# Transposes of two key blocks back to back in a causal attention kernel, value matmuls in pairs

## The chip, the cores and the metric

One core of one Trainium2 chip runs the whole program. The metric is the device time of one execution in microseconds (µs). Engines are named as in the profile: PE (TensorE, matmuls and transposes), PEld (its weight loads), DVE (VectorE), ACT (ScalarE), POOL (GpSimd), SP (the queue that issues the DMAs).

## The reference, cut to what matters

A layer norm with modulation, grouped causal attention, and a gated feed-forward part. The change touches the attention alone:

```python
qkv = einsum('bsh,ph->bsp', x, weight_qkv)       # b=2, s=1024, 4 kv groups, 4 query heads each, d=128
scores = einsum('bsgqd,btgd->bgqst', q, k) * scale
scores = where(causal, scores, min)
attn = softmax(scores, axis=-1)
out = einsum('bgqst,btgd->bsgqd', attn, v)
return einsum('bse,he->bsh', out, weight_proj)
```

## The kernel before

A program written by hand for each engine, with semaphores between them. The attention is a loop of 8 turns (batch x kv group, `t` = 0 to 7). Float32 products are made of two parts, a high one (`_hi`, type fp32r) and the rest (`_lo`), in three matmuls each (`three`, L801 to L806).

A turn has no loop inside. `walk()` writes out a list, and every engine goes through the same list `WALK` and does its own share of each item, strictly in that order:

- `C` n: a chunk of the q, k, v projection (6 matmuls, ACT and DVE make its high and low part).
- `S` i, h: scores of query block i (128 queries) of head h against keys 0 to (i+1)*128: 3 or 6 matmuls into a bank pair of `S`. DVE adds the mask to the diagonal block (L702) and takes the row maximum (L704), ACT takes the exponential (L487) with the row sum, POOL the reciprocal of the sum (L373) and the product with it (L378), in place in `prob`.
- `T` n: unit n = (i, j), query block i and key block j. The four heads' 128x128 blocks of `prob` are transposed by PE (L927) into one bank, `T[n % 2]`. ACT copies the bank to `pt_hi` (L506), DVE subtracts to make `pt_lo` (L709).
- `V` n: the three value matmuls of unit n (L804 to L806), added up in bank `O` over j. After the last of a row, ACT makes `o_hi` (L511) and DVE `o_lo` (L714).
- `Y` i: the output projection of row i (12 matmuls); DVE adds it to x (L720).

Rows go from block 7 (8 units, n = 0 to 7) down to block 0 (one unit, n = 35). The scores of row i-1 are spread over the units of row i by the table `SCORES_AT`.

What holds the order together:

- `T` n waits for `ptl_done` of unit n-2 (L919), since it overwrites the bank that unit's `pt_lo` is read from. At j = 0 it waits for `prob_done` of each head in turn (L926).
- `V` n waits for `ptl_done` of its own unit (L942).
- `S` waits until the exponential two scores earlier has emptied its banks (L900).
- ACT doesn't run the exponential of a score at its item. It keeps it in the list `waiting`, and runs it at the next `S` or `C` item, or behind the copy to `pt_hi` of the next `T` item (`exps`, L479, called at L501 and L507).
- Both T banks, all `S` banks and `O` fill PSUM, so there are two T banks only.

The names S61, T3 and so on below mean item `S` of row 6, head 1, and item `T` of unit 3.

Of the kernel before, what the change touches and what calls it, by code (L numbers as in the profile page):

```python
# [5 lines left out]
F32 = mybir.dt.float32  # L6
F32R = mybir.dt.float32r
ALU = mybir.AluOpType
ACT = mybir.ActivationFunctionType
AX = mybir.AxisListType  # L10

P = 128
B, SEQ, HID = 2, 1024, 256
NKV, QPG, D = 4, 4, 128
# [4 lines left out]
CH = 512  # L19
# [8 lines left out]
STEPS = [NT - 1 - s for s in range(NT)]  # L28
UNITS = [(i, j) for i in STEPS for j in range(i + 1)]
NU = len(UNITS)  # L30
LAST = {i: max(n for n, u in enumerate(UNITS) if u[0] == i) for i in STEPS}

SA, CA, GA, SB, CB, GB = range(6)
# [9 lines left out]
def walk():  # L43

    out = [("C", 0, 0), ("C", 1, 0), ("C", 2, 0), ("C", 3, 0), ("VT", 0, 0), ("C", 4, 0), ("C", 5, 0), ("L", 0, 0)]
    for h in range(QPG):
        out += [("S", STEPS[0], h), ("C", 6 + h, 0)]  # L50
    out += [("C", 10, 0), ("S", STEPS[1], 0), ("C", 11, 0)]
    lag = 2

    def values(n):
        out.append(("V", n, 0))
        i, j = UNITS[n]
        if i < STEPS[0] and j == min(PROJECT_AT, i):
            out.append(("Y", i + 1, 0))

    for n, (i, j) in enumerate(UNITS[:-1]):  # L60
        out += [("S", i - 1, h) for h in range(QPG) if (n or h) and SCORES_AT[i][h] == 2 * j]
        out.append(("T", n, 0))
        out += [("S", i - 1, h) for h in range(QPG) if (n or h) and SCORES_AT[i][h] == 2 * j + 1]
        if n >= lag:
            values(n - lag)

    out += [("V", NU - 3, 0), ("V", NU - 2, 0), ("T", NU - 1, 0), ("Y", 2, 0), ("V", NU - 1, 0), ("Y", 1, 0), ("Y", 0, 0)]
    return out


# [19 lines left out]
def build(nc, x_in, wqkv, wproj, wmod, c_cols, wug, wdn, su_ug, su_dp, ws_ug, ws_dp, ident_in, mask_in, had_in, out):  # L90
    ctx = ExitStack()
    with ctx:
        def sb(name, shape, dt=F32):
            return ctx.enter_context(nc.sbuf_tensor(name, shape, dt))
# [12 lines left out]
        v_hi = sb("v_hi", [P, NT, D], F32R)  # L107
        v_lo = sb("v_lo", [P, NT, D], F32R)
        prob = sb("prob", [P, 2, QPG, SEQ])
        pt_hi = sb("pt_hi", [P, 3, CH], F32R)  # L110
        pt_lo = sb("pt_lo", [P, 3, CH], F32R)
        o_hi = sb("o_hi", [P, 2, CH], F32R)
        o_lo = sb("o_lo", [P, 2, CH], F32R)
        w_raw = sb("w_raw", [P, KH, GW])
# [61 lines left out]
        S = [psum[0], psum[1]]  # L176
# [50 lines left out]
        def this(s, t, k):  # L227

            return (t + 1) * per[s.name] + k
# [188 lines left out]
        def _(act):  # L418
# [37 lines left out]
            with act.Fori(0, B) as b:  # L456
                with act.Fori(0, NKV) as g:
                    t = b * NKV + g

                    def v_high():  # L460
                        for n in range(2):
                            act.wait_ge(vtr_done, this(vtr_done, t, n + 1))
                            a_.activation(v_hi[:, 4 * n:4 * n + 4, :].rearrange("p j d -> p (j d)"), T[n],
                                          ACT.Copy).then_inc(v_hi_s, 1)

                    def chunk(c):
                        what, h, half = CHUNKS[c]
                        act.wait_ge(qkv_done, this(qkv_done, t, c + 1))
                        span = slice(half * CH, (half + 1) * CH)
                        if what == "v":  # L470
                            a_.activation(vt[:, span], bank(c), ACT.Copy).then_inc(vt_done, 1)
                        elif what == "k":
                            a_.activation(k_hi[:, span], bank(c), ACT.Copy).then_inc(qkv_hi, 1)
                        else:
                            a_.activation(q_hi[:, h, span], bank(c), ACT.Copy, scale=SCALE).then_inc(qkv_hi, 1)

                    waiting = []

                    def exps():  # L479

                        while waiting:
                            i, h = waiting.pop(0)
                            s = NT - 1 - i
                            nb, w = halves(i)

                            act.wait_ge(max_done, this(max_done, t, QPG * s + h + 1))
                            a_.activation(prob[:, s % 2, h, 0:nb * w].rearrange("p (a n) -> p a n", a=nb),  # L487
                                          score_banks(i, h).rearrange("p (a n) -> p a n", a=nb)[:, :, 0:w],
                                          ACT.Exp, bias=nmax[:, s % 2, h:h + 1],
                                          accum_out=rsum[:, s % 2, h:h + 1]).then_inc(exp_done, 1)  # L490

                    for what, n, h in WALK:
                        if what == "C":
                            chunk(n)
                            if n == 3:
                                v_high()
                            exps()
                        if what == "L":
                            ln_modulate(1, b, g, 0)
                        if what == "S":  # L500
                            exps()  # L501
                            waiting.append((n, h))
                        if what == "T":
                            act.wait_ge(t_done, this(t_done, t, n + 1))

                            a_.activation(pt_hi[:, n % 3, :], T[n % 2], ACT.Copy).then_inc(pth_done, 1)  # L506
                            exps()  # L507
                        if what == "V" and n == LAST[UNITS[n][0]]:
                            s = NT - 1 - UNITS[n][0]
                            act.wait_ge(pv_done, this(pv_done, t, n + 1))  # L510
                            a_.activation(o_hi[:, s % 2, :], O[s], ACT.Copy).then_inc(oh_done, 1)  # L511
# [53 lines left out]
        def _(dve):  # L565
# [96 lines left out]
            with dve.Fori(0, B) as b:  # L662
                with dve.Fori(0, NKV) as g:
# [21 lines left out]
                    for what, n, h in WALK:  # L685
                        if what == "C":
                            chunk(n)
                            if n == 3:
                                v_low()
                            if n == 0:  # L690
                                dve.wait_ge(add_done, this(add_done, t, 0))
                                ln_front(1, b, g, 0)
                            if n == 3:
                                ln_normalise(1, b, g, 0)
                        if what == "S":
                            s = NT - 1 - n
                            nb, w = halves(n)
                            dve.wait_ge(s_done, this(s_done, t, QPG * s + h + 1))

                            at = (nb - 1) * CH + w - P  # L700
                            diagonal = score_banks(n, h)[:, at:at + P]
                            v_.tensor_tensor(diagonal, diagonal, mask_f[:, :], ALU.add).then_inc(masked, 1)  # L702
                            dve.wait_ge(masked, this(masked, t, QPG * s + h + 1))
                            v_.tensor_reduce(nmax[:, s % 2, h:h + 1],  # L704
                                             score_banks(n, h).rearrange("p (a n) -> p a n", a=nb)[:, :, 0:w],
                                             AX.XY, ALU.max, negate=True).then_inc(max_done, 1)
                        if what == "T":
                            dve.wait_ge(pth_done, this(pth_done, t, n + 1))
                            v_.tensor_tensor(pt_lo[:, n % 3, :], T[n % 2], pt_hi[:, n % 3, :].bitcast(F32),  # L709
                                             ALU.subtract).then_inc(ptl_done, 1)  # L710
                        if what == "V" and n == LAST[UNITS[n][0]]:
                            s = NT - 1 - UNITS[n][0]
                            dve.wait_ge(oh_done, this(oh_done, t, s + 1))
                            v_.tensor_tensor(o_lo[:, s % 2, :], O[s], o_hi[:, s % 2, :].bitcast(F32),  # L714
                                             ALU.subtract).then_inc(ol_done, 1)
                        if what == "Y":
                            s = NT - 1 - n
                            dve.wait_ge(y_done, this(y_done, t, s + 1))
                            row = x[:, bass.ds(b * NT + n, 1), :].rearrange("p a n -> p (a n)")
                            v_.tensor_tensor(row, O[s][:, 0:HID], row, ALU.add).then_inc(add_done, 1)  # L720
# [74 lines left out]
        def _(pe):  # L795
# [57 lines left out]
            with pe.Fori(0, B) as b:  # L853
                with pe.Fori(0, NKV) as g:
# [30 lines left out]
                    for what, n, h in WALK:  # L885
# [43 lines left out]
                        if what == "V":  # L929
# [10 lines left out]
                            if n == 0:  # L940
                                pe.wait_ge(v_lo_s, this(v_lo_s, t, 2))
                            pe.wait_ge(ptl_done, this(ptl_done, t, n + 1))  # L942
                            three(O[s], v_hi[:, j, :], v_lo[:, j, :], pt_hi[:, n % 3, :], pt_lo[:, n % 3, :],
                                  j == 0, j == i).then_inc(pv_done, 1)
                        if what == "Y":
                            s = NT - 1 - n
# [131 lines left out]
```

## Time and profile before

| what | before |
| --- | --- |
| device time, median of 3 runs | 989.67 µs (989.23 to 989.75) |
| profiled execution, span from first to last instruction | 987.8 µs |
| busy PE, DVE, ACT, POOL in it | 948.2, 707.7, 521.1, 468.1 µs |
| one turn of attention (the second, trace time 129.22 to 229.46) | 100.24 µs |
| behind the last turn | 157.0 µs |

The span leaves out what lies around the first and the last instruction: the median is 1.9 µs above it. The starts of PE's rows are exact, the ends modelled and overlapping, so PE's pace is read from start to start, and a wait of PE as the part of such a distance that the same pair of instructions does not show elsewhere.

### The profile page before, as it was taken

Reading aid. Unit: us, or ns where it says so; the run is one execution under the profiler, and the core shown is the slowest. Engines: PE = TensorE matmul, PEld = TensorE weight load, DVE = VectorE, ACT = ScalarE, POOL = GpSimd, SP = SyncE. Lnnn points to the kernel's source line nnn. Section 1 sums busy time; section 2 is a strip of 40 time slices with the busy share of each in tenths; the row PEclk is TensorE's granted clock in tenths of the full one; section 3 lists DMA queues with packets and bytes.
Section 4 is the critical chain, followed back from the end, with each engine's and each line's share of the span. In section 5 each row is a group of like instructions: output and inputs, shape, how many; then the busy total and the mean of one; then the engine's idle time right before and its main releaser. Section 6 shows DMA issues by size and latency. Waiting matters only on the chain.

```text
span 987.8 us, 17271 instructions
## 1 busy us (share of the span) xinstructions
PE 948.2 (96%) x5344; PEld 815.3 (83%) x5344; DVE 707.7 (72%) x1290; ACT 521.1 (53%) x1085; POOL 468.1 (47%) x603
## 2 busy tenths in 40 slices
PE   6899999999999999999999999999999999999997
PEld 5688878887898789878987898779887987888885
DVE  6777767786778677857786778677767876864543
ACT  2466646664666466646664666466646665331221
POOL 4665546564555455545654565456555647120000
PEclk9999999999999999999999999999999999999999
DMA  8000000000000000000000000000000020000000
GB/s 293 22 1 34 1 21 0 32 0 21 0 32 0 21 0 32 0 21 0 32 0 21 0 32 0 7 14 32 0 0 0 0 85 0 1 2 21 21 21 22
DMA packets 9617, 20.80 MB, mean 21 GB/s; under 512 B 1280, under 2 KB 5632, under 8 KB 9472
## 3 DMA queue, kind: packets, MB, share of 16 engines
q1 hardware_dynamic: 8736, 20.45, 6.0%
q10 hardware_dynamic: 864, 0.15, 0.1%
q8 instruction: 8, 0.13, 0.1%
q14 instruction: 9, 0.07, 0.0%
HBM read 18.50 MB, written 2.10 MB: 21 GB/s over the span
## 4 chain that ended last, share of the span: by engine, by line
PE 79%; DVE 7%; issue 6%; POOL 3%; ACT 3%; DMA 0%; DVEq 0%; POOLq 0%; ACTq 0%; SPq 0%
PE ps L804 17%; PE ps L806 16%; PE ps L805 16%; PE ps L927 10%; PE ps L906 6%; PE ps L912 6%; PE ps L909 6%; POOL rinv L373 2%; DVE pt_lo L709 2%; POOL prob L378 2%; ACT prob L487 1%; DVE xhat L614 1%; PE ps L828 1%; DVE v_lo L681 1%; DVE ps L702 1%
## 5 line engine op out<-in xcount | busy, mean ns | idle before, releaser
L709 DVE TENSOR_TENSOR pt_lo<-ps,pt_hi 128x512 fp32r<-128x512 f32 x288 | 196.8, 686 | 69.6 <-ACT pt_hi L506 68.8
L373 POOL TENSOR_TENSOR rinv<-rsum,mone 128x1 f32<-128x1 f32 x256 | 140.8, 550 | 213.5 <-ACT prob L487 212.4
L487 ACT ACTIVATE prob<-ps,nmax 128x1024 f32<-128x1024 f32 (+7 forms) x256 | 190.0, 742 | 79.4 <-DVE nmax L704 77.8
L506 ACT ACTIVATE pt_hi<-ps 128x512 fp32r<-128x512 f32 x288 | 171.0, 597 | 108.3 <-PE ps L927 107.5
L378 POOL TENSOR_SCALAR prob<-prob,rinv 128x1024 f32<-128x1024 f32 (+7 forms) x256 | 192.2, 751 | 52.7 <-POOL rinv L373 52.7
L704 DVE TENSOR_REDUCE nmax<-ps 128x1 f32<-128x1024 f32 (+7 forms) x256 | 194.0, 758 | 8.7
L927 PE MATMUL ps<-ident,prob 128*128 128x128 f32 x1152 | 175.5, 274 | 10.3 <-DVE pt_lo L709 7.5
L927 PEld LDWEIGHTS ps<-ident,prob 128*128 128x128 f32 x1152 | 139.7, 140 | 43.4 <-DVE pt_lo L709 18.5
L804 PE MATMUL ps<-pt_hi,v_hi 128*128 128x512 f32 x288 | 132.5, 460 | 1.3 <-DVE pt_lo L709 0.5
L806 PE MATMUL ps<-pt_hi,v_lo 128*128 128x512 f32 x320 | 126.3, 395 | 0.0
L906 PE MATMUL ps<-k_hi,q_hi 128*128 128x512 f32 (+4 forms) x384 | 117.5, 360 | 0.0
L805 PE MATMUL ps<-pt_lo,v_hi 128*128 128x512 f32 x288 | 113.5, 394 | 0.0
L912 PE MATMUL ps<-k_hi,q_lo 128*128 128x512 f32 (+4 forms) x384 | 110.8, 343 | 0.0
L909 PE MATMUL ps<-k_lo,q_hi 128*128 128x512 f32 (+4 forms) x384 | 110.3, 341 | 0.0
L702 DVE TENSOR_TENSOR ps<-ps,mask_f 128x128 f32<-128x128 f32 x256 | 74.9, 293 | 20.9 <-PE ps L912 19.4
L804 PE MATMUL ps<-h_hi,w_hi 128*128 x192 | 76.2, 397 | 1.8 <-POOL h_lo L327 1.8
L906 PEld LDWEIGHTS ps<-k_hi,q_hi 128*128 128x128 f32 x384 | 68.2, 189 | 9.4
L909 PEld LDWEIGHTS ps<-k_lo,q_hi 128*128 128x128 f32 x384 | 70.7, 188 | 5.7
L805 PE MATMUL ps<-h_lo,w_hi 128*128 x192 | 75.3, 392 | 0.0
L806 PE MATMUL ps<-h_hi,w_lo 128*128 x192 | 75.2, 392 | 0.0
L912 PEld LDWEIGHTS ps<-k_hi,q_lo 128*128 128x128 f32 x384 | 70.6, 189 | 4.9
L804 PE MATMUL ps<-wp_hi,o_hi 128*128 128x256 f32 x256 | 73.7, 288 | 0.0
(134 smaller groups left out, 1613.6 us busy)
## 6 DMA issues: line engine op xcount, KB each, us to landing
w_raw<-in_wqkv SPq DMA_DIRECT2D x9, 768.0 KB, 4.3
wp_raw<-in_wproj SPq DMA_DIRECT2D x8, 512.0 KB, 3.4
x<-in_x SPq DMA_DIRECT2D x4, 512.0 KB, 8.9
prob<-in_wug SPq DMA_DIRECT2D x4, 512.0 KB, 5.4
out_y<-prob SPq DMA_DIRECT2D x4, 512.0 KB, 2.9
prob<-in_wmod SPq DMA_DIRECT2D x1, 1024.0 KB, 8.7
raw_down<-in_wdn SPq DMA_DIRECT2D x1, 1024.0 KB, 13.4
prob<-in_wmod SPq DMA_DIRECT2D x1, 512.0 KB, 4.9
```

What stands on the lines that cost most here:

```text
L378: g_.tensor_scalar(row, row, rinv[:, s % 2, h:h + 1], 1.0, ALU.mult, ALU.mult).then_inc(prob_done, 1)
L487: a_.activation(prob[:, s % 2, h, 0:nb * w].rearrange("p (a n) -> p a n", a=nb), score_banks(i, h).rearrange("p (a n) -> p a n", a=nb)[:, ...
L506: a_.activation(pt_hi[:, n % 3, :], T[n % 2], ACT.Copy).then_inc(pth_done, 1)
L704: v_.tensor_reduce(nmax[:, s % 2, h:h + 1], score_banks(n, h).rearrange("p (a n) -> p a n", a=nb)[:, :, 0:w], AX.XY, ALU.max, negate=True) ...
L709: v_.tensor_tensor(pt_lo[:, n % 3, :], T[n % 2], pt_hi[:, n % 3, :].bitcast(F32), ALU.subtract).then_inc(ptl_done, 1)
L804: mm(dst, w_h, r_h, start=start, stop=False)
L805: mm(dst, w_h, r_l, start=False, stop=False)
L806: return mm(dst, w_l, r_h, start=False, stop=stop)
L906: mm(dst[:, a * CH:a * CH + wide], q_hi[:, h, q_at], k_hi[:, a * w:a * w + wide], start=True, stop=False)
L909: mm(dst[:, a * CH:a * CH + wide], q_hi[:, h, q_at], k_lo[:, a * w:a * w + wide], start=False, stop=False)
L912: last = mm(dst[:, a * CH:a * CH + wide], q_lo[:, h, q_at], k_hi[:, a * w:a * w + wide], start=False, stop=True)
L927: last = tr(T[n % 2][:, h * P:(h + 1) * P], prob[:, s % 2, h, j * P:(j + 1) * P], ident[:, :])
```

## The change

`walk()` now takes the units of a row in pairs (`PAIRS`: units 0 and 1, 2 and 3, ...; a row with an odd number of units ends in a single one). For a pair, the transposes of both units stand next to each other, the scores that stood between them follow behind, and then come both value items of the pair before. `pt_hi` and `pt_lo` get 4 slots instead of 3. On ACT the last unit's item first empties the list of waiting exponentials. The program is built with a smaller scratch for descriptors of dynamic DMAs (1024), which makes room in SBUF.

```diff
+PAIRS = [[n for n in (m, m + 1) if n < NU and UNITS[n][0] == UNITS[m][0]] for m in range(NU) if UNITS[m][1] % 2 == 0]
...
-    for n, (i, j) in enumerate(UNITS[:-1]):
-        out += [("S", i - 1, h) for h in range(QPG) if (n or h) and SCORES_AT[i][h] == 2 * j]
-        out.append(("T", n, 0))
-        out += [("S", i - 1, h) for h in range(QPG) if (n or h) and SCORES_AT[i][h] == 2 * j + 1]
-        if n >= lag:
-            values(n - lag)
-
-    out += [("V", NU - 3, 0), ("V", NU - 2, 0), ("T", NU - 1, 0), ("Y", 2, 0), ("V", NU - 1, 0), ("Y", 1, 0), ("Y", 0, 0)]
+    def scores(n, at):
+        i, j = UNITS[n]
+        return [("S", i - 1, h) for h in range(QPG) if (n or h) and SCORES_AT[i][h] == 2 * j + at]
+
+    for p, pair in enumerate(PAIRS[:-1]):
+        out += scores(pair[0], 0)
+        out += [("T", n, 0) for n in pair]
+        out += scores(pair[0], 1)
+        for n in pair[1:]:
+            out += scores(n, 0) + scores(n, 1)
+        for n in PAIRS[p - 1] if p else ():
+            values(n)
+
+    out += [("V", n, 0) for n in PAIRS[-2]]
+    out += [("T", NU - 1, 0), ("Y", 2, 0), ("V", NU - 1, 0), ("Y", 1, 0), ("Y", 0, 0)]
...
-        pt_hi = sb("pt_hi", [P, 3, CH], F32R)
-        pt_lo = sb("pt_lo", [P, 3, CH], F32R)
+        pt_hi = sb("pt_hi", [P, 4, CH], F32R)
+        pt_lo = sb("pt_lo", [P, 4, CH], F32R)
...
                         if what == "T":
+                            if n == NU - 1:
+                                exps()
                             act.wait_ge(t_done, this(t_done, t, n + 1))
...
-    nc = bacc.Bacc("TRN2", target_bir_lowering=False, num_devices=1)
+    nc = bacc.Bacc("TRN2", target_bir_lowering=False, num_devices=1, dynamic_dma_scratch_size=1024)
```

The list reads so in the first row of a turn, before and with the change:

```text
before: T0 S61 T1 S62 T2 V0 T3 V1 T4 S63 V2 T5 V3 T6 V4 T7 V5 S50 T8 S51 V6 T9 S52 V7 T10 V8 S53 T11 V9 Y7
change: T0 T1 S61 S62 T2 T3 V0 V1 T4 T5 S63 V2 V3 T6 T7 V4 V5 S50 T8 T9 S51 S52 V6 V7 T10 T11 S53 V8 V9 Y7
```

PE in the first row, from S62 on, before (L906 to L912 scores, L927 transposes, L804 to L806 value matmuls, the x4 rows being the four heads of one unit):

```order
L906 MATMUL ps<-k_hi,q_hi 128x448 x2
L909 MATMUL ps<-k_lo,q_hi 128x448 x2
L912 MATMUL ps<-k_hi,q_lo 128x448 x2
L919 REGISTER_ALU
L927 MATMUL ps<-ident,prob 128x128 x4
L935 REGISTER_ALU
L804 MATMUL ps<-pt_hi,v_hi 128x512
L805 MATMUL ps<-pt_lo,v_hi 128x512
L806 MATMUL ps<-pt_hi,v_lo 128x512
L919 REGISTER_ALU
L927 MATMUL ps<-ident,prob 128x128 x4
```

The same place with the change (all lines of PE stand 9 lower):

```order
L915 MATMUL ps<-k_hi,q_hi 128x448 x2
L918 MATMUL ps<-k_lo,q_hi 128x448 x2
L921 MATMUL ps<-k_hi,q_lo 128x448 x2
L928 REGISTER_ALU
L936 MATMUL ps<-ident,prob 128x128 x4
L928 REGISTER_ALU
L936 MATMUL ps<-ident,prob 128x128 x4
L944 REGISTER_ALU
L813 MATMUL ps<-pt_hi,v_hi 128x512
L814 MATMUL ps<-pt_lo,v_hi 128x512
L815 MATMUL ps<-pt_hi,v_lo 128x512
```

The transposes of T3 have moved ahead of the value matmuls of V0.

DVE at the start of the same row, T0 to T2, before (L702 mask, L704 maximum, L709 low part):

```order
L709 TENSOR_TENSOR pt_lo<-ps,pt_hi 128x512
L698 REGISTER_ALU
L702 TENSOR_TENSOR ps<-ps,mask_f 128x128
L704 TENSOR_REDUCE nmax<-ps 128x1
L708 REGISTER_ALU
L709 TENSOR_TENSOR pt_lo<-ps,pt_hi 128x512
L698 REGISTER_ALU
L702 TENSOR_TENSOR ps<-ps,mask_f 128x128
L704 TENSOR_REDUCE nmax<-ps 128x1
L708 REGISTER_ALU
L709 TENSOR_TENSOR pt_lo<-ps,pt_hi 128x512
```

With the change:

```order
L718 TENSOR_TENSOR pt_lo<-ps,pt_hi 128x512
L717 REGISTER_ALU
L718 TENSOR_TENSOR pt_lo<-ps,pt_hi 128x512
L707 REGISTER_ALU
L711 TENSOR_TENSOR ps<-ps,mask_f 128x128
L713 TENSOR_REDUCE nmax<-ps 128x1
L707 REGISTER_ALU
L711 TENSOR_TENSOR ps<-ps,mask_f 128x128
L713 TENSOR_REDUCE nmax<-ps 128x1
L717 REGISTER_ALU
L718 TENSOR_TENSOR pt_lo<-ps,pt_hi 128x512
```

The low part of unit 1 now stands ahead of the maximum of S61, which it followed before.

ACT at the end of a turn, T33 to T35, before (L506 copies to `pt_hi`, L487 exponentials, here of S02 and S03, L511 the copies to `o_hi` of rows 2 and 1):

```order
L506 ACTIVATE pt_hi<-ps 128x512
L486 REGISTER_ALU
L487 ACTIVATE prob,rsum<-ps,nmax 128x128
L504 REGISTER_ALU
L506 ACTIVATE pt_hi<-ps 128x512
L486 REGISTER_ALU
L487 ACTIVATE prob,rsum<-ps,nmax 128x128
L511 ACTIVATE o_hi<-ps 128x512 x2
L504 REGISTER_ALU
L506 ACTIVATE pt_hi<-ps 128x512
```

With the change:

```order
L515 ACTIVATE pt_hi<-ps 128x512
L493 REGISTER_ALU
L494 ACTIVATE prob,rsum<-ps,nmax 128x128
L513 REGISTER_ALU
L515 ACTIVATE pt_hi<-ps 128x512
L520 ACTIVATE o_hi<-ps 128x512 x2
L493 REGISTER_ALU
L494 ACTIVATE prob,rsum<-ps,nmax 128x128
L513 REGISTER_ALU
L515 ACTIVATE pt_hi<-ps 128x512
```

The exponential of S03, which T35 transposes, has moved behind both copies to `o_hi`.

## Rows read from the trace of the kernel before

**Rows 1.** The page, part 1 and its DMA queues of part 3.

```profile
PE 948.2 (96%) x5344; PEld 815.3 (83%) x5344; DVE 707.7 (72%) x1290; ACT 521.1 (53%) x1085; POOL 468.1 (47%) x603
...
q1 hardware_dynamic: 8736, 20.45, 6.0%
```

**Rows 2.** Waits of PEld: total us, times, longest us.

```profile
PEld ps L927 <- DVE pt_lo L709: 18.5, 24, 1.0
...
PEld ps L927 <- POOL prob L378: 4.2, 8, 0.5
...
PEld ps L804 <- DVE pt_lo L709: 6.5, 16, 0.5
```

**Rows 3.** Timeline of PE: start us, us, instruction; early in turn 0, then turn 1.

```profile
29.98 1.03 PE L882 MATMUL ps<-ident,prob 128*128 128x128 f32 x8
...
173.05 0.60 PE L927 MATMUL ps<-ident,prob 128*128 128x128 f32 x4
173.40 0.48 PE L804 MATMUL ps<-pt_hi,v_hi 128*128 128x512 f32 x1
173.72 0.39 PE L805 MATMUL ps<-pt_lo,v_hi 128*128 128x512 f32 x1
173.95 0.40 PE L806 MATMUL ps<-pt_hi,v_lo 128*128 128x512 f32 x1
174.18 0.51 PE L906 MATMUL ps<-k_hi,q_hi 128*128 128x384 f32 x2
```

**Rows 4.** Timeline of all engines, first row of turn 1, units 0 to 4.

```profile
158.09 1.09 DVE L704 TENSOR_REDUCE nmax<-ps 128x1 f32<-128x896 f32 x1
...
159.07 0.40 PE L806 MATMUL ps<-pt_hi,v_lo 128*128 128x512 f32 x1
159.21 1.01 ACT L487 ACTIVATE prob<-ps,nmax 128x896 f32<-128x896 f32 x1 [1.46 <-DVE nmax L704]
...
159.83 0.66 PE L927 MATMUL ps<-ident,prob 128*128 128x128 f32 x4 [0.36 <-DVE pt_lo L709]
...
160.21 0.59 ACT L506 ACTIVATE pt_hi<-ps 128x512 fp32r<-128x512 f32 x1
...
161.02 0.68 DVE L709 TENSOR_TENSOR pt_lo<-ps,pt_hi 128x512 fp32r<-128x512 f32 x1
...
161.76 0.65 PE L927 MATMUL ps<-ident,prob 128*128 128x128 f32 x4 [0.57 <-DVE pt_lo L709]
```

**Rows 5.** Groups of instructions by line and form: busy us, mean ns.

```profile
L702 DVE TENSOR_TENSOR ps<-ps,mask_f 128x128 f32<-128x128 f32 x256 | 74.9, 293 | 20.9 <-PE ps L912 19.4
...
L378 POOL TENSOR_SCALAR prob<-prob,rinv 128x896 f32<-128x896 f32 x32 | 32.6, 1020 | 6.6 <-POOL rinv L373 6.6
...
L704 DVE TENSOR_REDUCE nmax<-ps 128x1 f32<-128x640 f32 x32 | 26.4, 824 | 1.1
...
L487 ACT ACTIVATE prob<-ps,nmax 128x640 f32<-128x640 f32 x32 | 25.6, 799 | 3.8 <-DVE nmax L704 3.8
```

**Rows 6.** Timeline, last rows of turn 1, units 33 to 35.

```profile
218.45 0.37 ACT L487 ACTIVATE prob<-ps,nmax 128x128 f32<-128x128 f32 x1 [1.40 <-DVE nmax L704]
...
218.99 0.55 POOL L373 TENSOR_TENSOR rinv<-rsum,mone 128x1 f32<-128x1 f32 x1 [1.14 <-ACT prob L487]
...
219.75 0.37 POOL L378 TENSOR_SCALAR prob<-prob,rinv 128x128 f32<-128x128 f32 x1 [0.21 <-POOL rinv L373]
...
223.14 0.39 PE L806 MATMUL ps<-pt_hi,v_lo 128*128 128x512 f32 x1
223.37 0.60 PE L927 MATMUL ps<-ident,prob 128*128 128x128 f32 x4
223.56 0.60 ACT L511 ACTIVATE o_hi<-ps 128x512 fp32r<-128x512 f32 x1 [0.94 <-PE ps L806]
```

**Rows 7.** Windows: us, busy us of each engine, granted clock (eighth); then timeline of PE.

```profile
30.00:50.00 20.00, 16.27 (x71) 13.07 (x70) 14.51 (x31) 9.79 (x18) 11.35 (x10) 0.91 0.07 27
...
37.49 0.63 PE L828 MATMUL ps<-ident,xhat 128*128 128x128 f32 x4 [3.73 <-DVE xhat L614]
```

More of the change, by code:

```diff
@@ L51, in walk @@
     out += [("C", 10, 0), ("S", STEPS[1], 0), ("C", 11, 0)]
-    lag = 2
     def values(n):
@@ L503, in _ @@
                         if what == "T":
+                            if n == NU - 1:
+                                exps()
                             act.wait_ge(t_done, this(t_done, t, n + 1))
-                            a_.activation(pt_hi[:, n % 3, :], T[n % 2], ACT.Copy).then_inc(pth_done, 1)
+                            a_.activation(pt_hi[:, n % 4, :], T[n % 2], ACT.Copy).then_inc(pth_done, 1)
                             exps()
@@ L708, in _ @@
                             dve.wait_ge(pth_done, this(pth_done, t, n + 1))
-                            v_.tensor_tensor(pt_lo[:, n % 3, :], T[n % 2], pt_hi[:, n % 3, :].bitcast(F32),
+                            v_.tensor_tensor(pt_lo[:, n % 4, :], T[n % 2], pt_hi[:, n % 4, :].bitcast(F32),
                                              ALU.subtract).then_inc(ptl_done, 1)
@@ L942, in _ @@
                             pe.wait_ge(ptl_done, this(ptl_done, t, n + 1))
-                            three(O[s], v_hi[:, j, :], v_lo[:, j, :], pt_hi[:, n % 3, :], pt_lo[:, n % 3, :],
+                            three(O[s], v_hi[:, j, :], v_lo[:, j, :], pt_hi[:, n % 4, :], pt_lo[:, n % 4, :],
                                   j == 0, j == i).then_inc(pv_done, 1)
```

## The prediction

> **What bounds the kernel now.** First the page: PE is busy 948.2 of 987.8 µs, the next engine, DVE, 707.7, and the DMA queue takes 6.0% of its engines [rows 1]. So the time is PE's own work plus its waits, and a change of order can only move the waits. Then the waits of PE's weight loads, which see a late operand first: in the attention loop transposes wait for `pt_lo` 24 times (3 a turn), the first matmul of a value item 16 times (2 a turn), a transpose for `prob` 8 times (once a turn) [rows 2]. Then the timeline of one turn from start to start, which gives the sizes per turn (a transpose group of four is 0.44, three value matmuls 0.69): T3 0.53+0.06, T4 0.74+0.06, T32 0.30, T33 0.45, V34 0.30, V35 0.43. That is 2.87 µs a turn, 23.0 µs over 8 turns, all that the change could take away of this kind. The wait in front of the layer norm's transposes, about 1 µs a turn, lies ahead of the first pair and stays.
>
> **The pair itself gives nothing on PE.** Four transposes take 0.35 µs to the start of the value matmul behind them; that one holds the next back by 0.32 where its neighbours take 0.23 [rows 3]. So the group costs 0.35+0.09 = 0.44. Eight transposes in a row, the projection's v blocks, take 1.03 less the 0.27 of the last one's own length, 0.76 for 7 steps, 0.109 each [rows 3], so eight are 0.87, twice 0.44. The longer first value matmul is the last transpose still running, not a price of changing kind. 16 fewer changes a turn gain 0. If the 0.09 were a price, they would gain 16 x 8 x 0.09 = 11.5 µs; I keep this for the range.
>
> **The fourth slot and the scratch.** Slots cost no instruction. Nothing waited for a `pt` slot before: the order alone protected it. The DMAs are few and hidden (6.0%). I take 0, for either sign.
>
> **What the pair does to the waits.** Before, between T n and T n+2, which share a bank, stood at least one value item or score on each side. Now T n+1 follows T n by 0.44, but its copy and its low part come one after the other, behind whatever ACT and DVE still owe. I replayed one turn, on the clock of turn 1 (first transposes at 154.85), in the new order of the list, with starts and lengths of this trace. Steps: last transpose to copy 0.31; copy 0.59; low part 0.68, next one 0.60 later; mask 0.29 and maximum [rows 4, 5]; semaphore 0.03 to 0.06. In the first row:
>
> - DVE now does the low part of unit 1 before the maximum of S61. Before, that maximum ran 158.09 to 159.18 [rows 4]; now it is 0.60 later, to 159.77.
> - ACT still runs that exponential (1.01) ahead of unit 2's copy: 159.81 to 160.82. Copy to 161.42, low part to 162.14. Before, copy at 160.21 and low part at 161.02 let T4 go at 161.76 [rows 4]. Now T4 goes at 162.20. PE has done T2, T3, V0, V1 by 160.43: it waits **1.77**.
> - Then ACT runs the exponential of S62 ahead of unit 3's copy: to 162.31, copy to 162.91, low part to 163.63. T5 goes at 163.69 instead of 162.64, a wait of **1.05**. Before, S63 and V2 stood between T4 and T5 and hid exactly this.
>
> So the first row waits 2.82 in place of 1.39.
>
> The end of the turn has the second large one. T35, the single unit of row 0, needs `prob` of S03. Before, its exponential stood right behind unit 34's copy. Now both copies to `o_hi` are ahead of it, and the second needs V34. ACT starts that copy 0.42 behind V34's last matmul [rows 6], 0.88 behind V34's start. Exponential 0.48 later, 0.37 long; 0.17 to the reciprocal; 0.76 from there to the product; product 0.37 [rows 6], and 0.06 to PE. Sum: 0.88+0.48+0.37+0.17+0.76+0.37+0.06 = 3.09 behind V34's start. PE would put T35's fourth transpose 0.69+0.33 = 1.02 behind it. Wait **2.07**. V35 then waits 0.14 for its low part, in place of 0.43. Nothing but these waits is queued on PE, and the next turn starts later by all of it.
>
> Between them, the scores. S42 now follows S41 with nothing in between and needs the exponential of S40, which stands behind unit 15's copy on ACT: 0.58 late. S43 needs that of S41: unit 16's copy is behind the exponential of S40 (0.80), its low part ahead of the mask and maximum (0.33 and 0.82) [rows 5], then again 0.80; with V14, T17 and T18 as the only cover, 0.77 late. The same happens smaller in row 6 (S52 0.24, S53 0.15; before, V6, V7 and V8 stood between). T8 waits 0.48 for the product of S63 (1.02) [rows 5], whose exponential now stands behind unit 6's copy; T21 waits 0.41 in the same way. In row 3, T29 waits 0.59 for unit 27's low part, and Y4 0.91 for `o_lo`, whose copy stands behind two exponentials. At the end T32 0.29, Y3 0.39, V33 0.60, V34 0.17.
>
> **Sum.** New waits of a turn: 2.82 + (0.48+0.24+0.15) + (0.58+0.77) + 0.41 + (0.59+0.91) + (0.29+0.39) + (0.60+0.17) + (2.07+0.14) = 10.61. Old ones gone: 2.87. Difference 7.74, x 8 = 61.9. Span 987.8+61.9 = 1049.7; the median lay 1.9 above the span, so 1051.6, called **1051**.
>
> Bounds. Each small wait is the difference of two chains and could be wrong by 0.1 to 0.2; if all twelve small ones from T8 to V34 came out at half (5.58 to 2.79), the sum is 4.95 x 8 = 39.6: 1029. If I read only the two big ones rightly (2.82-1.39 and 2.21-0.43), and the rest stayed as before, it is 3.21 x 8 = 25.7: 1015. With the 11.5 of above off the forecast: 1040. Upwards: the clock, below: 1065.
>
> **The clock.** Early in the trace PE waited 3.73 µs, and its clock then fell from 2.4 to 1.2 GHz: the granted clock is 0.91 over 30 to 50 µs, a loss of 0.09 x 20 / 0.5 = 3.6 µs at half speed, of which about half, 1.8, is lost [rows 7]. In the attention, waits of 1 µs in front of the transposes of each turn left it at 1.00. The new waits, 1.77 and 1.05 close together and 2.07, lie between. If one a turn had this effect: 8 x 1.8 = 14, so 1065. The Trainium skill (TensorE: Matmul & The Clock Gate, Part 4: PE-mode transpose) says that transposes don't count as work for the clock's monitor. By that, the stretch T4, wait, T5 would look idle throughout, and the clock could fall in every turn; eight transposes in a row [rows 3] did not show it here.
>
> **Rivals.**
> - *Slower as summed, 1029 to 1060*: 0.72. The order of each engine's list is certain and the lengths repeat within 0.01 from turn to turn.
> - *Slower, with the clock falling as well, 1060 to 1075*: 0.10.
> - *Slower, but only in the first row and at the last unit, 1010 to 1029*: 0.10. For it: ACT (53%) and DVE (72%) have room, and PE's waits let them catch up. Against it: the exponentials are late by order, not by load.
> - *Faster, 966 to 987*: 0.04. The mechanism: V n, V n+1 behind T n+2, T n+3 give unit n+1's chain (0.31+0.59+0.68+0.1 from its last transpose) a whole pair, 2.26 from T n+1 to T n+3, less the 0.33 of the group. 1.93 against 1.68 fits by 0.25. Where ACT and DVE have nothing else ahead, no transpose waits, and 2.87 x 8 = 23 µs goes: 966.7. It decides from 0.25 µs of foreign work in the chain on: an exponential of 0.80 to 1.01 or a maximum is above this in rows 7 to 4, where most pairs are.
> - *No change, within 0.2%*: 0.04: new waits just eat up the old ones, 2.87 a turn. It needs the T35 wait (2.07) plus 0.8 elsewhere to be all.
>
> 0.2% (2 µs) is about what a measurement of this kernel can tell from no change. The range leaves out the fast cases and the lower part of the third: 1022 to 1068.
>
> **What the changed profile would show.** The turn 108.0 long in place of 100.24, PE busy as before (948) in a longer span. PE's weight loads wait for `pt_lo` at T4 and T5 by about 1.8 and 1.0 each turn. A wait of about 2 of the turn's last transpose for POOL's `prob`. S42, S43 wait for ACT's exponentials. The granted clock 1.00. Behind the last turn 157 µs as before. The forecast is wrong if T4 and T5 don't wait longer than T3 and T4 did, or if the transpose groups standing together become shorter than 0.44.

## The result and the profile after

| what | before | changed |
| --- | --- | --- |
| device time, median | 989.71 µs (989.23 to 989.85, 4 runs) | 1063.64 µs (1062.56 to 1067.67, 4 runs) |
| ratio to before | 1 | 1.0754 (1.0734 to 1.0773) |
| span of the profiled execution | 987.8 µs | 1065.9 µs |
| mean granted clock (1 is 2.4 GHz) | 0.997 | 0.982 |
| PE, DVE, ACT, POOL busy | 948.2, 707.7, 521.1, 468.1 µs | 979.1, 712.2, 507.9, 466.7 µs |

The change makes the kernel 7.5% slower. The profiled execution is the slowest of the four; the others have a granted clock of 0.986. PE runs 5344 matmuls and transposes in both kernels. Its busy time is longer without more work: a row in front of a wait is counted with its whole length, of which the next row otherwise covers a part, and a fall of the clock makes rows longer.

Waits of PEld in the changed kernel (total µs, times, longest), against [rows 2]. All lines of PE stand 9 lower in the file than before.

```profile
PEld ps L936 <- DVE pt_lo L718: 35.0, 40, 2.0
PEld ps L936 <- POOL prob L385: 25.5, 24, 2.2
PEld ps L915 <- ACT prob L494: 14.4, 24, 0.7
```

Transposes waited 24 times for `pt_lo`, at most 1.0 µs, and 8 times for `prob`, at most 0.5. Now it is 40 times and up to 2.0, and 24 times and up to 2.2. Scores that wait for an exponential (L915) are new.

The timeline of the first row of turn 1, units 2 to 5, the place of [rows 4]:

```profile
169.18 1.29 DVE L718 TENSOR_TENSOR pt_lo<-ps,pt_hi 128x512 fp32r<-128x512 f32 x2 [0.78 <-ACT pt_hi L515]
...
170.18 1.04 PE L936 MATMUL ps<-ident,prob 128*128 128x128 f32 x8
...
170.71 1.09 DVE L713 TENSOR_REDUCE nmax<-ps 128x1 f32<-128x896 f32 x1
...
170.97 0.48 PE L813 MATMUL ps<-pt_hi,v_hi 128*128 128x512 f32 x1
...
171.83 1.01 ACT L494 ACTIVATE prob<-ps,nmax 128x896 f32<-128x896 f32 x1 [2.20 <-DVE nmax L713]
...
172.20 0.39 PE L815 MATMUL ps<-pt_hi,v_lo 128*128 128x512 f32 x1
...
172.83 0.59 ACT L515 ACTIVATE pt_hi<-ps 128x512 fp32r<-128x512 f32 x1
...
173.30 1.01 ACT L494 ACTIVATE prob<-ps,nmax 128x896 f32<-128x896 f32 x1
173.45 0.69 DVE L718 TENSOR_TENSOR pt_lo<-ps,pt_hi 128x512 fp32r<-128x512 f32 x1 [0.32 <-ACT pt_hi L515]
...
174.19 0.66 PE L936 MATMUL ps<-ident,prob 128*128 128x128 f32 x4 [1.60 <-DVE pt_lo L718]
174.29 1.20 ACT L515 ACTIVATE pt_hi<-ps 128x512 fp32r<-128x512 f32 x2
...
175.67 0.66 PE L936 MATMUL ps<-ident,prob 128*128 128x128 f32 x4 [0.82 <-DVE pt_lo L718]
```

The chain is to be read from the top. DVE makes the low parts of units 0 and 1 first (169.18), so that the maximum of S61 starts at 170.71, 3.84 behind T0 (166.87); before it was 3.24 (158.09 and 154.85). The exponential of S61 on ACT, which needs it, is later by the same 0.60. On PE, T2 and T3 are one row of eight transposes, and then come V0 and V1, the last matmul of which starts at 172.20. T4 could start 0.23 later, at 172.43, and starts at 174.19: it waits 1.76. Unit 2's copy (172.83) stands behind that exponential (171.83, 1.01), although its transposes were done by 171. Unit 3's copy is the first of the two at 174.29, behind the exponential of S62. T5 starts 1.48 behind T4. Without a wait of its own that would be 0.44, and 0.06 for the wait of T4 just before it; the rest, 0.98, is T5's wait. Eight transposes and the step behind them take 170.97-170.18 = 0.79, as in the v blocks of [rows 3]: standing together makes them no shorter.

The end of the same turn, the place of [rows 6]:

```profile
241.64 0.49 PE L936 MATMUL ps<-ident,prob 128*128 128x128 f32 x3
241.84 0.60 ACT L520 ACTIVATE o_hi<-ps 128x512 fp32r<-128x512 f32 x1 [1.28 <-PE ps L815]
242.33 0.36 ACT L494 ACTIVATE prob<-ps,nmax 128x128 f32<-128x128 f32 x1
...
244.13 0.38 PE L813 MATMUL ps<-wp_hi,o_hi 128*128 128x256 f32 x1
...
244.94 0.28 PE L813 MATMUL ps<-wp_hi,o_hi 128*128 128x256 f32 x1
...
245.41 0.42 PE L813 MATMUL ps<-wp_hi,o_hi 128*128 128x256 f32 x1
```

Three transposes of T35 run, the fourth needs S03's product, whose exponential runs only at 242.33 behind the copy to `o_hi`. The projection behind it starts at 244.13 and not at 242.0: 2.1 µs later. And then something that no wait explains: the same matmul takes 0.28 at 244.94 and 0.42 at 245.41. Windows of the changed kernel (µs, busy µs of each engine, then the granted clock): turn 1, turn 4, and the place itself.

```profile
141.28:250.74 109.46, 101.03 (x578) 86.18 (x577) 75.12 (x135) 57.47 (x126) 53.86 (x71) 0.98 0.04 12
...
243.00:248.60 5.60, 4.55 (x23) 4.27 (x24) 1.68 (x4) 1.19 (x2) 0.79 (x2) 0.70 0.00 0
```

```profile
470.62:579.33 108.71, 100.02 (x579) 84.83 (x577) 75.37 (x135) 57.47 (x126) 53.89 (x71) 1.00 0.04 12
```

Behind the wait of 2.1 the clock fell to 1.2 GHz: the granted clock of 0.70 over 5.6 µs makes 0.30 x 5.6 / 0.5 = 3.4 µs at this level. In this profile it fell so behind T4 and T5 in five of the eight turns (0, 2, 3, 5, 6) and behind T35 in four (0, 1, 6, 7). In turn 4 it did not, and this turn is 108.71 long, 8.24 above the same turn of the kernel before (100.47; the batch changes in it, and it is 0.3 longer than its neighbours there too).

### The profile page after: what moved, and what is told of

The parts are those of the page before. It is cut to its first block, busy times and chain, and to the rows that moved or that the text cites. A ratio compares the mean times of both kernels' runs of the same rounds, so it can differ in the third digit from the quotient of the medians.

```text
span 1065.9 us, 17271 instructions
## 1 busy us (share of the span) xinstructions
PE 979.1 (92%) x5344; PEld 828.3 (78%) x5344; DVE 712.2 (67%) x1290; ACT 507.9 (48%) x1085; POOL 466.7 (44%) x603
## 4 chain that ended last, share of the span: by engine, by line
PE 62%; DVE 13%; issue 10%; ACT 10%; POOL 3%; ACTq 0%; DVEq 0%; DMA 0%; POOLq 0%; SPq 0%
PE ps L813 15%; PE ps L815 14%; PE ps L814 14%; ACT prob L494 6%; PE ps L936 5%; PE ps L915 4%; PE ps L921 4%; PE ps L918 4%; DVE nmax L713 4%; ACT pt_hi L515 3%; DVE ps L711 2%; DVE pt_lo L718 2%; POOL prob L385 2%; POOL rinv L380 1%; DVE o_lo L723 1%
## 5 line engine op out<-in xcount | busy, mean ns | idle before, releaser
L936 PE MATMUL ps<-ident,prob 128*128 128x128 f32 x1152 | 162.9, 277 | 42.7 <-DVE pt_lo L718 22.2
L936 PEld LDWEIGHTS ps<-ident,prob 128*128 128x128 f32 x1152 | 132.9, 141 | 70.2 <-DVE pt_lo L718 35.0
L915 PE MATMUL ps<-k_hi,q_hi 128*128 128x512 f32 (+4 forms) x384 | 122.2, 373 | 7.7 <-ACT prob L494 7.2
L813 PE MATMUL ps<-pt_hi,v_hi 128*128 128x512 f32 x288 | 124.4, 432 | 3.2 <-DVE pt_lo L718 3.2
L918 PE MATMUL ps<-k_lo,q_hi 128*128 128x512 f32 (+4 forms) x384 | 112.6, 348 | 0.0
L915 PEld LDWEIGHTS ps<-k_hi,q_hi 128*128 128x128 f32 x384 | 68.3, 193 | 21.5 <-ACT prob L494 14.4
L813 PE MATMUL ps<-wp_hi,o_hi 128*128 128x256 f32 x256 | 76.6, 299 | 6.7 <-DVE o_lo L723 6.7
```

The source lines that it names most:

```text
L813: mm(dst, w_h, r_h, start=start, stop=False)
L915: mm(dst[:, a * CH:a * CH + wide], q_hi[:, h, q_at], k_hi[:, a * w:a * w + wide], start=True, stop=False)
L918: mm(dst[:, a * CH:a * CH + wide], q_hi[:, h, q_at], k_lo[:, a * w:a * w + wide], start=False, stop=False)
L936: last = tr(T[n % 2][:, h * P:(h + 1) * P], prob[:, s % 2, h, j * P:(j + 1) * P], ident[:, :])
```

## The experiments

Theory: the loss is the waits that follow from the order of the list on in-order engines, plus the clock that falls behind the long ones. Rivals: slots and memory layout; a price of the pairs themselves; a clock that falls for another reason. Each time is compared with the kernel before, run beside it on the same chip. Edits are shown against the changed kernel, unless said.

**Slots and scratch alone.** The changed kernel with the old order of `walk()`.

> The order of before with the changed kernel's four slots, its smaller DMA scratch and its early exponentials on ACT at unit 35. Theory (all of the loss is the order of the list): 989.7 us, within 2. Rival (slots, addresses or scratch carry a part of the loss): above 992.

Measured: 989.67 µs, ratio 1.0002 (0.9993 to 1.0012). A turn is 100.20 long. All of the loss is the order.

**Pairs in the first row only.**

```diff
-    for p, pair in enumerate(PAIRS[:-1]):
+    for p, pair in enumerate(PAIRS[:4]):
...
+    for n, (i, j) in list(enumerate(UNITS[:-1]))[8:]:
...
```

The loop over units 8 and up is the one of the kernel before.

> Pairs in the first row of each turn only (units 0 to 7), everything behind as before. Theory: waits of 1.77 at T4, 1.05 at T5 and 0.48 at T8 in place of 0.59 at T3 and 0.80 at T4, so 1.9 us a turn and 15 us in all: 1005 with the clock at 2.4 GHz throughout, up to 1011 if it falls behind T4 and T5 in some turns. Rival (the loss is spread over all pairs by their number, 4 of 16): 74 x 4/16 = 18, so 1008, but with waits of the same size at every pair.

Measured: 1007.82 µs, 1.0179 (1.0161 to 1.0197). A turn without a fall of the clock is 102.13 long, 1.93 more than before, 15.4 in all; the rest, 3, fits the two falls of the clock in the attention of its profile (1.3 in the turn from 654.49 to 757.92) and a longer slow stretch at the start. Its waits of PE:

```profile
PE ps L943 <- DVE pt_lo L725: 19.4, 16, 1.6
```

16 waits are two a turn, at T4 (1.76) and T5 (0.98); T8 waits 0.47. The other pairs of the row, T0 T1, T2 T3 and T6 T7, don't wait. The rival that spreads the loss evenly named nearly the same time, 1008; these unequal waits are what speaks against it.

**The waits filled with matmuls.**

```diff
                         if what == "T":
...
+                            for _ in range({4: 7, 5: 4, 35: 9}.get(n, 0)):
+                                mm(T[0] if n == 35 else X[1], v_hi[:, 0, :], k_hi[:, 0:CH], start=True, stop=True)
```

> The changed kernel, with needless matmuls of 512 columns into a free bank while PE would wait: 7 ahead of T4, 4 ahead of T5, 9 ahead of T35 (1.6, 0.9 and 2.0 us of the waits of 1.8, 1.0 and 2.1). Their results are overwritten. Theory (these waits make the clock fall, and that is what the time holds beyond the waits): the granted clock stays at 1.0 in the attention, turns of 108.0 to 108.3 us, 1050 to 1053. Rival (the time beyond the waits is something else, or the clock falls for the many small waits): 1060 or more, the clock still falling.

Measured: 1055.31 µs, 1.0660 (1.0642 to 1.0677). The waits are there as before the edit (T4 1.77, T5 0.99, T35 2.08), now filled. From one turn's layer norm transposes to the next:

```profile
148.63:257.13 108.50, 104.41 (x597) 88.59 (x597) 75.09 (x136) 57.56 (x126) 54.01 (x71) 1.00 0.04 12
```

PE does 20 needless matmuls more in each turn and the kernel is 8.3 µs faster than the changed one. The clock does not fall in the attention any more, and the turns are as long as the one of the changed kernel without a fall (108.41 to 108.50 here and 108.40 there between the same places), so that the fill itself costs next to nothing. So the falls cost 8 µs, and the waits the rest: 1055.3-989.4 = 65.9, 8.24 a turn. That is 2.3 µs above the top of what I expected; the waits, not the clock, were undersized.

**The last score earlier.**

```diff
-             3: (0, 0, 2, 3), 2: (0, 0, 0, 2), 1: (0, 0, 0, 2)}
+             3: (0, 0, 2, 3), 2: (0, 0, 0, 2), 1: (0, 0, 0, 0)}
```

> The changed kernel with score S03 ahead of T33 instead of behind T34, so that its exponential runs ahead of unit 34's copy and both copies to o_hi. Theory: the wait of 2.08 at T35 shrinks to about 0.3, V33 waits 0.5 longer, 1.2 us less a turn and 10 us less in all from the waits, and up to 12 more from the clock no longer falling behind T35: 1042 to 1054. Rival (T35's wait is covered again by a later one, or the clock falls elsewhere): 1060 to 1064.

Measured: 1051.55 µs, 1.0634 (1.0613 to 1.0655). T35 waits 0.24+0.06 (2.08+0.06 before the edit) and V33 1.08 (0.56). Two turns of it, without and with a fall of the clock:

```profile
353.13:460.23 107.10, 100.03 (x579) 84.86 (x577) 75.07 (x135) 57.59 (x126) 53.82 (x71) 1.00 0.03 12
```

```profile
244.46:353.13 108.67, 101.61 (x579) 86.10 (x577) 75.18 (x135) 57.58 (x126) 53.84 (x71) 0.98 0.04 12
```

No fall is left behind T35; behind T4 and T5 the clock falls in five of eight turns, as it did in the changed kernel. A fall costs 108.67-107.10 = 1.57 µs there. Behind T35 it costs 109.43-108.40 = 1.03 in the changed kernel (from one turn's layer norm transposes to the next, turn 1 against turn 4), in part because the wait that otherwise follows at Y0 (0.14, and 0.11 behind it) is gone in the slow turn.

**Both copies of a pair ahead of the exponential.**

```diff
-                    for what, n, h in WALK:
+                    for at, (what, n, h) in enumerate(WALK):
...
                             a_.activation(pt_hi[:, n % 4, :], T[n % 2], ACT.Copy).then_inc(pth_done, 1)
-                            exps()
+                            if WALK[at + 1][0] != "T":
+                                exps()
```

> The changed kernel, but on ACT the waiting exponential runs behind the second copy of a pair instead of between the two. Theory (the second unit of a pair is late because its copy stands behind an exponential): T5's wait of 1.05 shrinks to about 0.2 and T29's 0.5 to 0.1, while the exponentials come later and T8, S52 and T21 wait 0.5 longer each; about 1.1 us less a turn, 8 to 9 us less in all: 1050 to 1056 with some falls of the clock left. Rival (the low part on DVE or the bank is what T5 waits for): T5 still waits 1 us, 1063.

Measured: 1051.48 µs, 1.0617 (1.0601 to 1.0633). The first wait of its PEld is now for POOL's `prob`:

```profile
PEld ps L937 <- POOL prob L385: 33.0, 24, 2.1
```

T5 waits 0.11+0.06 in place of 0.98, so an exponential of 1.01 between two copies was what T5 waited for. T29 (0.05 for 0.54), S43 (0 for 0.73) and Y3 (0 for 0.33) gain too. And the exponentials, now later, are missed elsewhere: T8 0.97 (0.48), S52 0.73 (0.24), T21 0.90 (0.41), S42 0.80 (0.57). The turn without a fall is 107.30, 1.1 less than with the change. T4 still waits 1.76 in every turn, with T5 now right behind it, and in this profile the clock falls behind neither; behind T35's 2.08 it falls in six of eight turns. Neither order of the copy and the exponential serves a pair well.

**Value items in pairs, scores left in place.**

```diff
-        out += scores(pair[0], 0)
-        out += [("T", n, 0) for n in pair]
-        out += scores(pair[0], 1)
-        for n in pair[1:]:
-            out += scores(n, 0) + scores(n, 1)
+        for n in pair:
+            out += scores(n, 0)
+            out.append(("T", n, 0))
+            out += scores(n, 1)
```

> One half of the change alone: both value items of the pair before stand behind the second transposes, but the scores stay where they were, between the transposes of a pair where the table puts them there. Theory (what hurts most is that the scores have left the place between the transposes): T3 waits about 1.3, T4 and T5 0.1 each, S52 and S42 0.6, T29 0.9, T35 0.6; 4.0 to 4.3 us a turn more than before: 1022 to 1030. Rival (the value matmuls in pairs carry the loss): 1050 or more.

Measured: 1020.53 µs, 1.0310 (1.0294 to 1.0326). A turn:

```profile
236.94:341.10 104.16, 99.41 (x578) 84.85 (x577) 74.20 (x135) 58.62 (x126) 53.96 (x71) 1.00 0.04 13
```

This is 1.5 below the bottom of what I expected; the rival of 1050 falls. T3 waits 1.23, T29 0.86, S52 0.72, S42 0.67, T35 0.49; no fall of the clock in the attention. Of 74 µs, 31 come with the value items moved, 35 more of waits with the scores taken out from between the transposes, and 8 with the clock. Both halves carry about the same; that the scores are the worse half holds only with the clock counted to them.

**Before, with one projection later.** Against the kernel before:

```diff
     out += [("V", NU - 3, 0), ("V", NU - 2, 0), ("T", NU - 1, 0), ("Y", 2, 0), ("V", NU - 1, 0), ("Y", 1, 0), ("Y", 0, 0)]
+    out.remove(("Y", 4, 0))
+    out.insert(out.index(("S", 1, 2)) + 1, ("Y", 4, 0))
```

> The kernel before, with the projection of row 4 moved behind the first three scores of row 1 instead of ahead of them. Theory (T33's wait of 0.45 and T32's of 0.3 come from a chain on ACT, DVE and POOL that starts with these scores): both waits go, 0.7 us a turn, 984 us, 0.6% faster than before. Rival (POOL is late for other reasons): 989.7.

Measured: 983.92 µs, 0.9940 (0.9926 to 0.9953). The turn is 99.39 long and PEld's waits for `prob` (8 of them, 4.2 µs, in [rows 2]) are gone, as expected.

**A written order.** The same method forwards: the four slots, and the list moved item by item until the replay of one turn (done by a small program from here on, with the same lengths as in the prediction) shows almost no wait. It begins `T0 T1 S61 V0 T2 T3 S62 V1 T4 S63 T5 V2 T6 V3 V4 V5 T7 S50` and ends `V31 T33 V32 T34 Y3 V33 T35 V34 Y2 V35 Y1 Y0`.

> The changed kernel's slots with an order written out item by item, so that between two transposes of the same bank there are always about 2 us of scores or value matmuls and each score comes early enough: of the waits of before only about 1.0 us at V0 is left in the attention. Theory (the waits follow from order and lengths alone): 1.4 to 1.5 us a turn less than before, 978 us, 1.2% faster. Rival (waits come back elsewhere): 985 or more.

Measured: 982.00 µs, 0.9922 (0.9908 to 0.9936): faster by 0.8%, but 4 µs short of what I expected. Its waits of PE show one that was not in the replay:

```profile
PE ps L803 <- DVE x L719: 5.7, 8, 0.7
```

V33 is the first value item of row 1 and writes the bank of row 3's output. It waits until DVE has added Y3, and Y3 stood directly ahead of it: 0.88 a turn.

**The second written order.** With that wait in the replay (Y4 and Y3 are moved ahead of S02, and other places change as well): `T0 T1 S61 T2 S62 V0 T3 T4 V1 V2 T5 S63 V3 T6 V4 T7 V5 S50` to `T32 S00 S01 Y4 Y3 S02 T33 V30 S03 T34 V31 V32 V33 T35 V34 Y2 V35 Y1 Y0`.

> A second order written out item by item. In the first one, V33 waited 0.88 us for DVE to take row 3's projection out of the bank that V33 writes (Y3 stood directly ahead), which the replay had left out. Here Y4 and Y3 stand ahead of S02, six items earlier. Theory: this wait goes, 98.5 us a turn, about 13 us less than before in all: 975 to 978. Rival (something else holds V33 or the items behind it): 982 as the first.

Measured: 974.88 µs, 0.9848 (0.9834 to 0.9861), the fastest of all: 1.5% faster than before, and 0.1 µs below the range I expected. The turn is 0.99 shorter than in the first written order (99.33). V33's wait of 0.87, with the 0.1 behind it, is what goes; in the first row T2 now waits 0.96, where V0 waited 0.96. A turn:

```profile
227.09:325.43 98.34, 96.71 (x578) 85.06 (x577) 73.78 (x135) 58.91 (x126) 54.08 (x71) 1.00 0.04 13
```

It still has transposes side by side at several places (T0 T1, T3 T4, T8 T9, T11 T12, T16 T17, T18 T19), there where the list around them covers the chain.

## Why the prediction was right, point by point

- *PE bounds the kernel, and only waits can move.* Right: with slots and scratch alone nothing changed (989.67 beside 989.43), and the kernels differ by their waits, with DVE's and ACT's busy time nearly the same. PE's busy time was forecast to stay at 948 and is 979.1; turn 4, without a fall of the clock, has 100.02 in place of 97.89 for the same instructions.
- *The pair gives nothing on PE.* Right: eight transposes and the step behind them take 0.79 in both kernels. The gain of 11.5 that I kept in the range does not exist.
- *The waits at the named places.* Predicted and measured, from start to start and without what comes behind them: T4 1.77 and 1.76, T5 1.05 and 0.98, T8 0.48 and 0.48, S42 0.58 and 0.57, S43 0.77 and 0.73, T21 0.41 and 0.41, T29 0.59 and 0.54, Y4 0.91 and 0.83, Y3 0.39 and 0.33, V33 0.60 and 0.56, T35 2.07 and 2.08. The smaller ones come out too, but for V34, 0.17 forecast and 0.03 measured. No place was missing that mattered. The rival by which only the first row and the last unit wait falls by them: the other places make about half of the new waits, as forecast. The cause was shown for T5 (the exponential behind the copy) and T35 (the position of S03); for the others it is read from the timeline.
- *The sum, 7.74 a turn, 61.9.* Measured with the waits filled: 8.24 a turn, 65.9. The term that was undersized is the length of each wait: it was counted as the time until the next instruction may start, and nothing behind that. In the changed kernel the group of instructions that waited then also runs longer than the same group elsewhere: T4, T5 and T29 by 0.06, S42, S43 and V33 by 0.10, Y4 (1.53 for 1.43) by 0.10, Y3 (1.53 for 1.42) by 0.11. The old waits were counted with this, the new ones without it. Over the sixteen places it is about 1.1 a turn (8.24 and the old 2.87, less the lengths of 10.0). It is partly hidden in the total, since the forecast lengths themselves add up to 10.61 where 10.0 was measured: the two errors together leave the 0.5. The trace shows the weight load of T4 starting with its matmul, at 174.19, where it otherwise starts ahead; that this makes the group longer is likely, not shown.
- *The clock.* This part was wrong. The profile was to show a granted clock of 1.00, and the case with a fall had a chance of 0.10 and 14 µs; the clock fell in seven of eight turns of the profile and cost 8.3 µs at the median. The forecast had it unlikely because waits of 1 µs had left the clock alone. Waits of 1.76 and 0.98 close together were followed by a fall in 12 of 24 turns (five in the changed kernel, five with the last score earlier, two with pairs in the first row only), and the wait of 2.08 in 10 of 16. The price of 1.8 for a fall was half of 3.6 µs; the slow stretch is 3.4 µs, and it costs 1.57 behind T4 and T5 and 1.03 behind T35. The value items in pairs, with no wait above 1.3, had none. The Trainium skill (TensorE: Matmul & The Clock Gate, Part 4: PE-mode transpose) says that the full clock doesn't engage for transposes, which don't count as busy in the same way; with the copies first, T4 and T5 stood next to each other behind a wait of 1.76, and no fall came there in eight turns. That doesn't contradict the page, as matmuls stood around them, but a pair of transposes behind such a wait did not bring a fall by itself.
- *The median.* 1051 was forecast for the case without the clock and 1065 with it; 1063.6 lies in between, and the difference of 12.6 is 4.0 of undersized waits, 8.3 of clock, and 0.3 left over. So the case given 0.72 (1029 to 1060, no fall) did not come, and the one given 0.10 (1060 to 1075, slower as summed and the clock falling) did. The range of 1022 to 1068 was right because it kept room for a clock that was thought unlikely; the sum of the waits alone lay 12.6 below the measured time. That this sum came out to 6% is owed to the replay; that the falls, whose number nothing in the working gave, left the time inside the range is in part luck.
- *The rivals of the other sign* fell as written: the chain of the second unit of a pair fits only without foreign work ahead of it. There is truth in them too: in the changed kernel itself T3, T6 and T7 don't wait, and the second written order has six pairs of neighbours that don't.

## What to carry to other kernels

In a list that every engine walks in order, an item's price is not its length but what it stands in front of: replay one period with lengths from the trace, with every wait in it, bank reuse included. The replay named eleven waits to within 0.1 µs; the one by program missed the one wait that it had left out, and with it found an order that is 1.5% faster. With two buffers in rotation, what counts is the work between two users of the same buffer: it has to cover the copy and the low part behind the first of them. Grouping work on the bound engine was worth nothing here, since the group costs the same, and it took away the cover of the second one's chain.

## What the runs showed of the hardware

- A wait of PE costs 0.06 (transposes of a unit) to 0.10 or 0.11 µs (scores, value matmuls, projections) more than its length, seen in the length of the group that waited against the same group elsewhere.
- Waits of 1.76 and 0.98 µs, parted by one group of transposes, or one of 2.08 µs, were followed by 3.4 µs at 1.2 GHz in some turns of a kernel and not in others with the same instructions and the same waits to within 0.01 µs. A wait of 1.76 without the second one behind it was followed by none in eight turns. Filling the waits with matmuls that nobody reads kept 2.4 GHz and made the kernel 8.3 µs faster. What decides between the turns was not tested and stays open.
- In the first turn the granted clock fell in every kernel, for 3.4 µs in some profiles, as behind the 3.73 µs of [rows 7], and twice as long in others. Between two profiles with the same order, before and slots alone, the turn with the longer stretch is 105.99 long in place of 104.79.
